# Fused Flamingo layer pair on one core: weight loads of the context stage issued by GpSimd, ternary halves laid out as 2 KB runs in DRAM

## Chip, core and metric

The kernel runs on one core of one Trainium2 chip. The metric is the device time of one execution in microseconds, the median of several runs; lower is better. The profile is of one execution.

## What is computed

Two gated layers over x (4 x 512 x 512) with a context of 4 x 1024 x 512:

```
x = x + tanh(g_xattn[0]) * L0_xattn(layernorm(x), ctx, mask)       # softmax readout of the context
x = x + tanh(g_ffn[0])   * L0_ffn(layernorm(x), router, wg, wu, wd)  # 8 experts, ternary weights
x = x + tanh(g_xattn[1]) * L1_xattn(layernorm(x), ctx, Wq, Wk, Wv, Wo)  # 16 heads
x = x + tanh(g_ffn[1])   * L1_ffn(layernorm(x), w1, b1, w2, b2)      # 8 experts, gelu
```

What the change touches is the preparation of the first feed-forward's weights, 3 matrices of 512 x 512 for each of 8 experts:

```
def _weight_quant(w):
    s = 1.0 / jnp.clip(jnp.mean(jnp.abs(w)), EPS, None)
    return jnp.clip(jnp.round(w * s), -1.0, 1.0) / s
xq @ wq.T
```

Each matrix is scaled by its mean magnitude, rounded to -1, 0 or 1, and needed transposed.

## The kernel before

The program is a row of phases with a barrier between them: context, readout, router, mixture, gather, query, attention, output, expert. The order within a phase is written out by hand: each engine has its own in-order list, and semaphores tie the lists together. DMAs issued by one engine go into that engine's queue.

**The context phase** (`context_phase`) is a pipeline of 64 steps s = 8q + n. Step s does one product of 12 matmuls of 128x512 on TensorE (`gemm`, L354 and L357): for n below 4 a block of K for block q of the context, else a block of V. ScalarE and VectorE (`evacuate`) take it out of PSUM as a high and a low bf16 half, and SyncE stores both (`store`, L125 keys and L128 values). Beside that, four steps of eight each split one tile of a later context block into halves (L203, L267) and transpose one (`prepare`, L342; copied out by L207 and L271). The first three blocks j = 0, 1, 2 (the weights Wk, Wv and the first context block) and j = 3 are split and transposed before the first step; `load_ctx(j, slot)` (L118) loads a block of 1 MB into one of two buffers as soon as block j-1 is split.

**The ternary weights** ride in the same steps. Matrix i (24 of them, 1 MB in float32) is loaded into slot i % 3 of `w32` (which lies in `xres`) by `load_weights(i)` on SyncE (L134). At step 2i ScalarE sums its magnitudes (`total`, L232); at step 2i+2 TensorE adds the partition sums (L365) and VectorE makes the ternary values (`ternary`, L288 to L298, the last of which increments the semaphore `cast`). After that the slot is free, and `load_weights(i+3)` waits for just this: `sp.wait_ge(cast, i - 2)`. The matrix is transposed in two halves h = 2i, 2i+1 at steps s = h+5: TensorE transposes half h (`w_transposes`, L374) into the one buffer `psW`, ScalarE copies it to buffer h % 2 of `wout` (`w_copy`, L225), and SyncE stores it to DRAM (`store_weights`, L140, 256 KB). ScalarE's `w_copy(h)` waits until the store of half h-2 has landed (semaphore `w_stored`); TensorE's transposes of half h+1 wait for `w_copy(h)`. Step s of SyncE's list is: `store(s)`, which waits for VectorE's `evacuate` of step s; `store_weights(s-5)`; then on even steps `load_weights`, which waits for `ternary`. ScalarE's step is: copy of a context transpose, `w_copy`, on even steps `total`, `evacuate`, split.

In DRAM the ternary weights lie as `wt_dram[expert, partition, matrix, k, 512]`. A half is 256 of the last 512 columns for each of the four k, so its store writes four runs of 512 B per partition. The router phase fetches an expert with 12 KB per partition (`fetch`, L768) into `wT` of the same layout, and the mixture phase multiplies with `wT[:, e, m, k, :]` as the moving operand (`weights_of`, L1134, used at L1142 and L1157).

GpSimd sets four small constants at the start of the context phase (L108 to L113) and is then idle until the next phase.

Of the kernel before, what the change touches and what calls it, by code (L numbers as in the profile page):

```python
# [5 lines left out]
F32 = mybir.dt.float32  # L6
# [5 lines left out]
P = 128  # L12
# [5 lines left out]
E = 8  # L18
# [12 lines left out]
def context_phase(nc, sem, ctx, wk, bk, wv, keys_dram, values_dram, ident, ctxN, ctxT, x, xres, moments,  # L31
# [12 lines left out]
    with ExitStack() as c:  # L44
# [60 lines left out]
        with nc.Block() as block:  # L105
            @block.gpsimd
            def _(pool):
                nc.gpsimd.memset(ident[:, :], 0.0).then_inc(ident_zero, 1)  # L108
                pool.wait_ge(ident_zero, 1)
                nc.gpsimd.affine_select(out=ident[:, :], in_=ident[:, :], compare_op=ALU.not_equal, fill=1.0,  # L110
                                        base=0, pattern=[[-1, P]], channel_multiplier=1).then_inc(ident_ready, 1)
                nc.gpsimd.memset(vst[:, :, :, 2 * HD:VW], 1.0).then_inc(ones_set, 1)
                nc.gpsimd.memset(onesf[:, :], 1.0).then_inc(onesf_set, 1)  # L113

            @block.sync
            def _(sp):
# [13 lines left out]

                def load_weights(i):
                    if i >= 3:
                        sp.wait_ge(cast, i - 2)
                    sp.dma_start(w32[:, i % 3, :, :], weights[i % 3][i // 3].rearrange("(u p) d -> p u d", p=P)  # L134
                                 ).then_inc(w_loaded[i % 3], 16)

                def store_weights(h):
                    i, r = divmod(h, 2)
                    sp.wait_ge(w_copied, h + 1)
                    sp.dma_start(wt_dram[i // 3, :, i % 3, :, r * 2 * P:(r + 1) * 2 * P],  # L140
                                 wout[:, r, :, :]).then_inc(w_stored[r], 16)
# [23 lines left out]
                load_ctx(2, 0)  # L165
                for i in range(3):
                    load_weights(i)
                load_ctx(3, 1)
                load_ctx(4, 0)
                for s in range(8 * NQ):  # L170
# [3 lines left out]
                    if (h := half_at(s)) is not None:  # L174
                        store_weights(h)
                    if (i := summed_at(s)) is not None and i + 3 < NW:
                        load_weights(i + 3)
                    for b in range(B):
# [487 lines left out]
def router_phase(nc, sem, router_w, wt_dram, means, ident, xres, moments, wT, scales, expert_of, place, dispatch_dram):  # L666
# [5 lines left out]
    with ExitStack() as c:  # L672
# [55 lines left out]
        with nc.Block() as block:  # L728
            @block.gpsimd
            def _(pool):  # L730
# [10 lines left out]
                done(nc.gpsimd.tensor_tensor(rstd[:, :], veps[:, :], half[:, :], ALU.pow))  # L741
                nc.gpsimd.memset(wT[:, E - 2:E, :, :, :], 0.0).then_inc(zero_set, 1)
                pool.wait_ge(zero_set, 1)
# [22 lines left out]
            def _(sp):  # L766
                def fetch(e):
                    sp.dma_start(wT[:, e, :, :, :].rearrange("p m k d -> p (m k d)"),  # L768
                                 wt_dram[e].rearrange("p m k d -> p (m k d)")).then_inc(w_fetched, 16)

# [3 lines left out]
                sp.dma_start(dispatch_dram.rearrange("(p n) d -> p (n d)", p=P),  # L774
                             wT[:, E - 2:E, :, :, :].rearrange("p e m k d -> p (e m k d)")[:, 0:NS * DW].bitcast(F32)).then_inc(zero_stored, 16)
                for e in range(E):
# [180 lines left out]
def mixture_phase(nc, sem, ident, wT, scales, expert_of, dispatch_dram, mixture_dram):  # L957
# [3 lines left out]
    with ExitStack() as c:  # L961
# [32 lines left out]
        with nc.Block() as block:  # L994
# [129 lines left out]
            def _(pe):  # L1124
# [7 lines left out]
                def weights_of(j):  # L1132
                    e = nc.tensor.value_load(expert_of[0:1, bass.ds(j, 1)], min_val=0, max_val=E - 1)
                    return lambda m, k: wT[:, bass.ds(e, 1), m, k, :].rearrange("p o d -> p (o d)")  # L1134

# [1095 lines left out]
def flamingo_kernel(nc, a, out):  # L2231
# [8 lines left out]
    values_dram = dram("values", (B, T, NH * VW), BF16)  # L2240
    wt_dram = dram("ternary", (E, P, 3, KC, D), BF16)
    used = []
# [5 lines left out]
    with ExitStack() as c:  # L2248
# [12 lines left out]
        with ExitStack() as moe:  # L2261
            wT = moe.enter_context(nc.sbuf_tensor("wT", [P, E, 3, KC, D], BF16))
            scales = moe.enter_context(nc.sbuf_tensor("scales", [P, 2, NT + E - 1], F32))
# [63 lines left out]
```

## Time and profile before

| | us |
|---|---|
| median of 3 runs (range) | 1882.03 (1881.41 to 1887.19) |
| profiled execution | 1875.83 |
| its span | 1874.1 |
| TensorE busy, mean granted clock | 1468.3, 0.894 |
| VectorE busy | 1261.1 |
| ScalarE busy | 955.2 |
| GpSimd busy | 387.8 |
| context phase, start to the readout's first instruction | 0 to 319.9 |

Engines: PE is TensorE's matmuls, PEld its weight loads, DVE VectorE, ACT ScalarE, POOL GpSimd, SP SyncE; "SPq" is the time that SyncE's sequencer takes for a DMA issue. A row of waits says who waited for whom. Clock and DMA share are fractions of full speed and of 16 DMA engines.

### The profile page before, as it was taken

To read this page: it belongs to the slowest core of one execution; us is meant where nothing else is said; L and a number is where in the kernel's file an instruction comes from. 1 tells how busy PE (TensorE), PEld (TensorE's weight loads), DVE (VectorE), ACT (ScalarE), POOL (GpSimd) and SP (SyncE) were. 2 spreads that over 40 slices of the span, in tenths; PEclk is the share of its full clock that TensorE was granted. 3 is DMA by queue.
4 is the path that set the end of the run, shared out by engine and by line. 5 is a ranking of instruction groups with operands and counts; after the bars stand their busy time and mean duration, and the time that the engine had idled before them with its cause. 6 is when DMAs were issued, how large, how long until landed. Compare 5 with 4: busy or idle time off the path is not lost. (4 is left out here: it accounts for less than half of the span.)

```text
span 1874.1 us, 26625 instructions
## 1 busy us (share of the span) xinstructions
PE 1468.3 (78%) x8457; PEld 806.2 (43%) x8536; DVE 1261.1 (67%) x1528; ACT 955.2 (51%) x1426; POOL 387.8 (21%) x279
## 2 busy tenths in 40 slices
PE   4777877999933574277899999999945679999996
PEld 3444443455412232142344444444412356667663
DVE  3765664655576476744999999999837867665561
ACT  4655652344324453231477676777732277666551
POOL 0000000000032002500355555555663100000000
PEclk8989889999965798577799999999977779999998
DMA  6787756000035123822042424242138277666640
GB/s 213 229 258 243 233 189 219 1 0 0 1 146 218 63 87 107 207 63 79 10 108 75 106 72 110 71 108 70 31 123 230 106 263 246 215 225 232 228 154 29
DMA packets 168979, 251.54 MB, mean 134 GB/s; under 512 B 11321, under 2 KB 86073, under 8 KB 167745
## 3 DMA queue, kind: packets, MB, share of 16 engines
q1 hardware_dynamic: 166848, 244.21, 41.4%
q0 software_dynamic: 2048, 6.33, 1.1%
q8 instruction: 41, 0.67, 0.2%
q14 instruction: 42, 0.34, 0.1%
HBM read 180.23 MB, written 70.07 MB: 134 GB/s over the span
## 5 line engine op out<-in xcount | busy, mean ns | idle before, releaser
L1607 ACT ACTIVATE t_e<-t_psE 128x512 f32<-128x512 f32 x512 | 304.4, 597 | 138.2 <-PE t_psE L1702 113.3
L1646 DVE TENSOR_REDUCE t_nmax<-t_psM 128x1 f32<-128x1024 f32 x256 | 301.4, 1212 | 19.6 <-PE t_psM L1683 19.5
L1565 POOL TENSOR_TENSOR t_low<-t_e 128x1024 bf16<-128x1024 f32 x128 | 250.0, 1955 | 201.8 <-ACT t_e L1607 188.3
L1713 PE MATMUL t_psO<-t_e,vst 128*96 128x512 bf16 x512 | 199.6, 390 | 2.5 <-POOL t_low L1565 2.5
L1702 PE MATMUL t_psE<-t_qst,kst 99*128 99x512 bf16 x512 | 195.0, 382 | 5.6 <-ACT t_e L1607 5.4
L1713 PE MATMUL t_psO<-t_low,vst 128*96 128x512 bf16 x512 | 193.1, 377 | 0.0
L1654 DVE TENSOR_TENSOR t_low<-t_e 128x1024 bf16<-128x1024 f32 x128 | 173.6, 1357 | 24.2 <-ACT t_e L1607 23.9
L1683 PE MATMUL t_psM<-kst,t_qst 96*128 96x512 bf16 x512 | 164.1, 404 | 31.7 <-DVE t_nmax L1646 22.7
L2196 PE MATMUL e_psG<-xeT,e_w1p 128*128 (+1 forms) x1536 | 172.8, 276 | 9.8 <-DVE e_hT L2140 5.2
L2211 PE MATMUL e_psO<-e_w2p,e_hT 128*128 128x512 bf16 x752 | 164.9, 379 | 0.8
L2196 PEld LDWEIGHTS e_psG<-xeT,e_w1p 128*128 128x128 bf16 x1536 | 151.7, 99 | 31.3 <-issue 6.3
L2211 PEld LDWEIGHTS e_psO<-e_w2p,e_hT 128*128 128x128 bf16 x768 | 75.2, 98 | 88.9
L354 PE MATMUL c_psG<-ctxT,c_wT 128*128 128x512 bf16 x369 | 94.6, 408 | 2.2 <-DVE c_vst L280 0.9
L357 PE MATMUL c_psG<-c_wT,ctxT 128*128 128x512 bf16 x371 | 92.7, 401 | 0.9 <-issue 0.2
L1683 PEld LDWEIGHTS t_psM<-kst,t_qst 96*128 96x128 bf16 x512 | 47.2, 99 | 106.7 <-DVE t_nmax L1646 48.3
L225 ACT COPY c_wout<-c_psW 128x1024 bf16<-128x1024 bf16 x48 | 48.7, 1015 | 83.9 <-DMA ternary<-c_wout 82.9
L1713 PEld LDWEIGHTS t_psO<-t_e,vst 128*96 128x96 bf16 x512 | 63.1, 123 | 64.8 <-POOL t_low L1565 6.3
L638 PE MATMUL a_psR<-ctxN,a_pT 128*128 (+1 forms) x375 | 85.7, 384 | 4.3 <-DVE xres L551 3.9
L2092 ACT CAST e_w2p<-xres 128x2048 bf16<-128x2048 f32 x32 | 60.7, 1897 | 53.1 <-PE e_psO L2211 36.6
L616 PE MATMUL a_psS<-ctxT,a_xT 128*128 (+1 forms) x375 | 86.5, 385 | 0.6 <-issue 0.2
L2132 DVE TENSOR_TENSOR e_w1p<-piece,e_w1p 128x2048 bf16<-128x2048 f32 x32 | 72.2, 2287 | 18.5 <-ACT e_w1p L2087 18.5
L2098 ACT ACTIVATE e_g<-e_psG,e_b1T 128x256 f32<-128x256 f32 x128 | 53.6, 470 | 60.0 <-PE e_psG L2196 39.6
(228 smaller groups left out, 2238.1 us busy)
## 6 DMA issues: line engine op xcount, KB each, us to landing
piece<-in_L_ffn_w SPq DMA_DIRECT2D x32, 1024.0 KB, 13.7
xres<-in_L_ffn_w SPq DMA_DIRECT2D x32, 1024.0 KB, 15.2
values<-c_vst SPq DMA_DIRECT2D x32, 384.0 KB, 4.8
ternary<-c_wout SPq DMA_DIRECT2D x48, 256.0 KB, 5.5
wT<-ternary SPq DMA_DIRECT2D x8, 1536.0 KB, 23.5
kst<-keys SPq DMA_DIRECT2D x96, 128.0 KB, 4.0
vst<-values SPq DMA_DIRECT2D x16, 768.0 KB, 8.3
mixed<-t_ost SPq DMA_DIRECT2D x64, 192.0 KB
```

The lines of the kernel that those rows point to most:

```text
L354: last = nc.tensor.matmul(psG[:, k, :], wT[:, 0, a, k * P:(k + 1) * P], ctxT[:, b, q * 512:(q + 1) * 512], start=(i == 0), stop=(i == 11))
L357: last = nc.tensor.matmul(psG[:, k, :], ctxT[:, a, q * 512 + k * P:q * 512 + (k + 1) * P], wT[:, 1, b, :], start=(i == 0), stop=(i == 11))
L616: last = nc.tensor.matmul(psS[:, par, h * 512:(h + 1) * 512], xT[:, par, ra * KC + k, :], ctxT[:, rb * KC + k, bass.ds(b * T + h * 512, 512)],
L1565: nc.gpsimd.tensor_tensor(low[:, slot(h, u), :, :], e32[:, slot(h, u), :, :], upper(h, u), ALU.subtract).then_inc(lo_pool, 1)
L1607: nc.scalar.activation(e32[:, slot(h, u), i, :], psE[:, i, :], ACT.Exp, scale=SC).then_inc(expd, 1)
L1646: nc.vector.tensor_reduce(nmax[:, h // G % 2, h % G, u:u + 1], banks_of(place_of_max(b, m)).rearrange("p a t -> p (a t)"), AX_X, ALU.max, ...
L1654: nc.vector.tensor_tensor(low[:, slot(h, u), :, :], e32[:, slot(h, u), :, :], upper(h, u), ALU.subtract).then_inc(lo_dve, 1)
L1683: last = nc.tensor.matmul(banks_of(place_of_max(b, m))[:, i, :], qst[0:KR, g, h % G, u * P:(u + 1) * P], kst[0:KR, g, h % G, i * 512:(i + ...
L1702: nc.tensor.matmul(psE[:, i, :], kst[:, g, h % G, k * P:(k + 1) * P], qst[:, g, h % G, :], start=True, stop=True).then_inc(scored, 1)
L1713: last = nc.tensor.matmul(psO[0:VW, h % 2, :], vst[:, g, 2 * u + i, h % G, :], part[:, i, :], start=(u == 0 and i == 0 and r == 0), stop=( ...
L2196: last = nc.tensor.matmul(psG[:, g % 4, i, :], w1p[:, ra, k, f:f + P], xeT[:, rb * KC + k, ee, :].rearrange("p o s -> p (o s)"), start=(n ...
L2211: last = nc.tensor.matmul(psO[:, m, :], hT[:, ra, k, m * P:(m + 1) * P], w2p[:, rb, k, :], start=(k == 0 and i == 0), stop=(k == FC - 1 an ...
```

## The change

The weight loads of all 24 matrices move from SyncE's list to the end of GpSimd's. GpSimd first waits until the first context block has landed (`rows_loaded[0]` at 32), issues three loads, then one for each count of `cast`, the same semaphore and count as before. SyncE's list loses them and is otherwise the same. In DRAM and in `wT` the dimension of the half stands ahead of k, so a half is 1024 values, one run of 2 KB per partition; the mixture's moving operand becomes two runs of 256 values with 1024 from one to the next.

```diff
@@ context_phase, gpsimd
+                pool.wait_ge(rows_loaded[0], 32)
+                for i in range(NW):
+                    if i >= 3:
+                        pool.wait_ge(cast, i - 2)
+                    nc.gpsimd.dma_start(w32[:, i % 3, :, :], weights[i % 3][i // 3].rearrange("(u p) d -> p u d", p=P)
+                                        ).then_inc(w_loaded[i % 3], 16)
@@ context_phase, sync
-                def load_weights(i):
-                    if i >= 3:
-                        sp.wait_ge(cast, i - 2)
-                    sp.dma_start(w32[:, i % 3, :, :], weights[i % 3][i // 3].rearrange("(u p) d -> p u d", p=P)
-                                 ).then_inc(w_loaded[i % 3], 16)
-
                 def store_weights(h):
                     i, r = divmod(h, 2)
                     sp.wait_ge(w_copied, h + 1)
-                    sp.dma_start(wt_dram[i // 3, :, i % 3, :, r * 2 * P:(r + 1) * 2 * P],
+                    sp.dma_start(wt_dram[i // 3, :, i % 3, r, :, :],
                                  wout[:, r, :, :]).then_inc(w_stored[r], 16)
...
                 load_ctx(2, 0)
-                for i in range(3):
-                    load_weights(i)
                 load_ctx(3, 1)
...
-                    if (i := summed_at(s)) is not None and i + 3 < NW:
-                        load_weights(i + 3)
@@ mixture_phase, tensor
-                    return lambda m, k: wT[:, bass.ds(e, 1), m, k, :].rearrange("p o d -> p (o d)")
+                    return lambda m, k: wT[:, bass.ds(e, 1), m, :, k, :].rearrange("p o r d -> p (o r) d")
@@ flamingo_kernel
-    wt_dram = dram("ternary", (E, P, 3, KC, D), BF16)
+    wt_dram = dram("ternary", (E, P, 3, 2, KC, D // 2), BF16)
-            wT = moe.enter_context(nc.sbuf_tensor("wT", [P, E, 3, KC, D], BF16))
+            wT = moe.enter_context(nc.sbuf_tensor("wT", [P, E, 3, 2, KC, D // 2], BF16))
```

SyncE's list from the first context load on, before (`c_rows<-in_ctx` is a context load, `xres<-in_L_ffn_w*` a weight load, `ternary<-c_wout` a half's store):

```order
L118 DMA c_rows<-in_ctx 128x4x512 [waits c_lo_done]
L134 DMA xres<-in_L_ffn_wg 128x4x512
L134 DMA xres<-in_L_ffn_wu 128x4x512
L134 DMA xres<-in_L_ffn_wd 128x4x512
L118 DMA c_rows<-in_ctx 128x4x512 [waits c_lo_done] x3
L125 DMA keys<-c_kst 128x2x512 [waits c_lo_out] x3
```

and around steps 15 to 18, before:

```order
L134 DMA xres<-in_L_ffn_wg 128x4x512 [waits c_cast]
L128 DMA values<-c_vst 128x1536 [waits c_lo_out]
L140 DMA ternary<-c_wout 128x4x256 [waits c_w_copied]
L118 DMA c_rows<-in_ctx 128x4x512 [waits c_lo_done]
L125 DMA keys<-c_kst 128x2x512 [waits c_lo_out]
L140 DMA ternary<-c_wout 128x4x256 [waits c_w_copied]
L134 DMA xres<-in_L_ffn_wu 128x4x512 [waits c_cast]
```

The same two places of SyncE's list in the changed kernel:

```order
L124 DMA c_rows<-in_ctx 128x4x512 [waits c_lo_done] x4
L131 DMA keys<-c_kst 128x2x512 [waits c_lo_out] x4
```

```order
L134 DMA values<-c_vst 128x1536 [waits c_lo_out]
L140 DMA ternary<-c_wout 128x1024 [waits c_w_copied]
L124 DMA c_rows<-in_ctx 128x4x512 [waits c_lo_done]
L131 DMA keys<-c_kst 128x2x512 [waits c_lo_out]
L140 DMA ternary<-c_wout 128x1024 [waits c_w_copied]
```

GpSimd's list in the changed kernel, from the last constant to the fifth load (the row of `c_onesf` was the last of this phase before):

```order
L113 MEMSET c_onesf 128x128
L118 DMA xres<-in_L_ffn_wg 128x4x512 [waits c_rows_loaded0]
L118 DMA xres<-in_L_ffn_wu 128x4x512
L118 DMA xres<-in_L_ffn_wd 128x4x512
L118 DMA xres<-in_L_ffn_wg 128x4x512 [waits c_cast]
L118 DMA xres<-in_L_ffn_wu 128x4x512 [waits c_cast]
```

The loads left SyncE's list, where each stood between a store and the next step's stores, and stand alone in GpSimd's. The lists of TensorE, VectorE and ScalarE hold the same instructions in the same order.

## Rows read from the trace of the kernel before

**Rows 1.** Waits, 0 to 400 us: who waited for whom, total us, times, longest
```profile
ACT c_wout L225 <- DMA ternary<-c_wout: 82.9, 30, 9.0
...
PE c_psW L374 <- ACT c_wout L225: 48.3, 16, 5.1
```
**Rows 2.** Timeline of ScalarE, evacuations of steps 8 and 40: start, us, what
```profile
74.18 0.69 ACT L214 ACTIVATE c_kst<-c_psG,c_bias 128x512 bf16<-128x512 f32 x1 [1.07 <-PE c_psG L354]
...
231.83 0.68 ACT L214 ACTIVATE c_kst<-c_psG,c_bias 128x512 bf16<-128x512 f32 x1
```
**Rows 3.** Stretches: length, busy PE, PEld, DVE, ACT, POOL, then clock, DMA share, GB/s
```profile
111.00:150.00 39.00, 30.23 (x195) 16.56 (x197) 24.96 (x34) 23.69 (x30) 0.00 (x0) 0.91 0.78 243
150.00:192.00 42.00, 30.66 (x203) 17.27 (x205) 25.06 (x34) 24.25 (x33) 0.00 (x0) 0.92 0.76 242
```
**Rows 4.** Timeline of SyncE from 148 us, steps 23 to 28
```profile
148.19 0.37 SPq L134 DMA_DIRECT2D xres<-in_L_ffn_wu  x1
148.79 0.35 SPq L128 DMA_DIRECT2D values<-c_vst  x1
149.19 0.43 SPq L140 DMA_DIRECT2D ternary<-c_wout  x1
149.66 1.35 SPq L118 DMA_DIRECT2D c_rows<-in_ctx  x1
...
159.99 0.47 SPq L140 DMA_DIRECT2D ternary<-c_wout  x1
165.84 0.47 SPq L140 DMA_DIRECT2D ternary<-c_wout  x1
...
173.40 1.40 SPq L140 DMA_DIRECT2D ternary<-c_wout  x1
```
**Rows 5.** Timeline of ScalarE, `w_copy` of steps 25 and 28; in brackets idle before
```profile
157.15 1.01 ACT L225 COPY c_wout<-c_psW 128x1024 bf16<-128x1024 bf16 x1 [6.21 <-DMA ternary<-c_wout]
...
168.86 1.01 ACT L225 COPY c_wout<-c_psW 128x1024 bf16<-128x1024 bf16 x1 [0.99 <-DMA ternary<-c_wout]
```
**Rows 6.** Timeline of TensorE from 149 us
```profile
149.71 0.61 PE L374 MATMUL c_psW<-ident,xres 128*128 128x128 bf16 x8
150.16 2.75 PE L354 MATMUL c_psG<-ctxT,c_wT 128*128 128x512 bf16 x12
...
153.19 0.33 PE L365 MATMUL c_psA<-c_absum,c_onesf 128*128 128x1 f32 x2
158.31 1.01 PE L374 MATMUL c_psW<-ident,xres 128*128 128x128 bf16 x8 [4.78 <-ACT c_wout L225]
159.54 3.61 PE L354 MATMUL c_psG<-ctxT,c_wT 128*128 128x512 bf16 x11 [0.22 <-DVE c_kst L277]
```
**Rows 7.** DMA to landing, line 140 (ternary halves, 256 KB, runs of 512 B)
```profile
DMA to landing us min/median/max: 2.6/5.5/10.3
```
**Rows 8.** DMA to landing, tile c_kst (keys, 256 KB, runs of 1 KB)
```profile
DMA to landing us min/median/max: 2.1/4.2/10.4
```
**Rows 9.** DMA to landing, line 134 (weight loads, 1 MB)
```profile
DMA to landing us min/median/max: 5.5/6.2/12.0
```
**Rows 10.** Timeline of the start, SyncE and ScalarE
```profile
12.98 0.38 SPq L118 DMA_DIRECT2D c_rows<-in_ctx  x1
...
18.43 2.18 ACT L203 CAST ctxN<-c_rows 128x512 bf16<-128x512 f32 x4 [1.33 <-DMA c_rows<-in_ctx]
...
29.28 2.18 ACT L203 CAST ctxN<-c_rows 128x512 bf16<-128x512 f32 x4 [5.61 <-DMA c_rows<-in_ctx]
...
36.67 1.91 ACT L232 ACTIVATE ctxT<-xres 128x2048 bf16<-128x2048 f32 x1
```
**Rows 11.** GpSimd issues a DMA of 128 rows, timeline at 596 us
```profile
596.29 0.97 POOL L759 DMA_INDIRECT dispatch<-r_disp,place  x1 [0.30 <-issue]
```
**Rows 12.** Tile g_rows: GpSimd's DMA issues, VectorE's work beside them, ns min/median/max
```profile
L1192 POOL DMA_INDIRECT g_rows<-mixture,place x16: 947/1104/1234, 736.8 to 757.9; - x16
L1199 DVE SCALAR_TENSOR_TENSOR xres<-g_rows,gates,xres x16: 733/750/753, 740.2 to 761.8; 128x512 f32<-128x512 f32 x16
```
**Rows 13.** Timeline: load of matrix 11, the sum that needs it, its last ternary pass
```profile
129.08 0.37 SPq L134 DMA_DIRECT2D xres<-in_L_ffn_wd  x1
...
139.87 1.91 ACT L232 ACTIVATE ctxT<-xres 128x2048 bf16<-128x2048 f32 x1
...
154.61 1.23 DVE L298 TENSOR_SCALAR xres<-xres 128x2048 bf16<-128x2048 f32 x1
```
**Rows 14.** Tiles xres and c_rows: VectorE's work on 2048 and on 512 float32, ns
```profile
L294 DVE TENSOR_SCALAR xres<-xres x24: 1226/1227/1227, 50.1 to 274.5; 128x2048 f32<-128x2048 f32 x24
...
L267 DVE TENSOR_TENSOR ctxN<-c_rows,ctxN x40: 677/681/693, 10.5 to 259.9; 128x512 bf16<-128x512 f32 x40
```
**Rows 15.** Groups of the mixture, 620 to 736 us: busy, mean ns, idle before
```profile
L1142 PE MATMUL m_psG<-wT,m_xT 128*128 x178 | 45.2, 395 | 16.8 <-ACT m_xT L1026 14.9 <-DVE m_prod L1084 1.0 <-issue 0.7
```

More of the change, by code:

```diff
@@ L741, in _ @@
                 done(nc.gpsimd.tensor_tensor(rstd[:, :], veps[:, :], half[:, :], ALU.pow))
-                nc.gpsimd.memset(wT[:, E - 2:E, :, :, :], 0.0).then_inc(zero_set, 1)
+                nc.gpsimd.memset(wT[:, E - 2:E, :, :, :, :], 0.0).then_inc(zero_set, 1)
                 pool.wait_ge(zero_set, 1)
@@ L767, in fetch @@
                 def fetch(e):
-                    sp.dma_start(wT[:, e, :, :, :].rearrange("p m k d -> p (m k d)"),
-                                 wt_dram[e].rearrange("p m k d -> p (m k d)")).then_inc(w_fetched, 16)
+                    sp.dma_start(wT[:, e, :, :, :, :].rearrange("p m r k d -> p (m r k d)"),
+                                 wt_dram[e].rearrange("p m r k d -> p (m r k d)")).then_inc(w_fetched, 16)
                 sp.wait_ge(consts, ROWS_ZERO)
@@ L774, in _ @@
                 sp.dma_start(dispatch_dram.rearrange("(p n) d -> p (n d)", p=P),
-                             wT[:, E - 2:E, :, :, :].rearrange("p e m k d -> p (e m k d)")[:, 0:NS * DW].bitcast(F32)).then_inc(zero_stored, 16)
+                             wT[:, E - 2:E, :, :, :, :].rearrange("p e m r k d -> p (e m r k d)")[:, 0:NS * DW].bitcast(F32)).then_inc(zero_stored, 16)
                 for e in range(E):
```

## Prediction

> **What bounds the kernel now.** I read the waits first. The largest of the context stage is ScalarE's `w_copy`, which waits 82.9 us for stores of ternary halves to land; behind it TensorE waits 48.3 us, in 16 waits, for ScalarE to empty the one transpose buffer [rows 1]. The reader is to see that a DMA's landing, not its traffic, holds up the matmuls. Next the pace: steps 8 to 40 take 231.83 - 74.18 = 157.65 us, so a pair of steps (one matrix) takes 9.85 us [rows 2]. The stretches say what is not the bound: per 39 to 42 us TensorE is busy 30, VectorE 25, ScalarE 24, and the DMA engines 0.76 to 0.78 [rows 3].
>
> Then the timeline of one stall. At 148.19 SyncE issues a weight load of 1 MB, at 148.79 a store of values, at 149.19 a ternary half [rows 4]. That half lands when `w_copy` of step 25 starts, at 157.15: 7.96 us later, of which ScalarE sat idle 6.21 [rows 5]. TensorE's next transposes come at 158.31, after 4.78 us idle, and run at half rate (1.01 us where 0.61 stood before; then 3.61 us for 11 matmuls against 2.75 for 12) [rows 6]. So each long wait costs about 1.5 us more in clock.
>
> This closes into a loop per parity of step. Odd steps: from the start of `w_copy` at 157.15 to the next odd store at 159.99 go 2.84 us (copy, evacuation by ScalarE and VectorE, issue), so a pair takes at least L + 2.84, with L the time from issue to landing. By the pace, L is 9.85 - 2.84 = 7.0 on average. Even steps also hold the 1.9 us `total`: from the store of 165.84 the wait ends at 168.86 (L = 3.0), and the next even store is issued 4.54 us later, at 173.40, so L + 4.54 = 7.6 at the shortest [rows 4, 5]. TensorE's own floor per pair is 2 x 2.75 + 2 x 0.61 + 0.33 + 0.61 (one context transpose set on average) = 7.66 us [rows 6].
>
> **The change, part by part.** *The load leaves SyncE's queue.* SyncE's issues of 0.37 us are off the path: it mostly waits for VectorE. What counts is the place of the load in the queue. In the example it stood 1 us ahead of the half and held the odd half up. A load's minimum to landing is 5.5 us, a half's 2.6 and a keys store's 2.1 [rows 7 to 9]; at the start five transfers of 1 MB, issued from 12.98, are all in by 29.28, so 1 MB occupies the DMA engines for at most 16.3 / 5 = 3.3 us [rows 10]. In a queue of its own it can no longer delay the stores by that whole; it can share the engines with them. No row shows two queues at once, so I bound it. Best: no interference, odd L = 7.0 - 3.3 = 3.7. Worst: it goes first all the same, 7.0. In between, with equal turns, store and half (about 2 us of work together) take twice their time: 3.7 + 2 = 5.7.
>
> *Runs of 2 KB.* Keys with 1 KB runs land 0.5 us sooner at best than halves of the same 256 KB with 512 B runs [rows 7, 8]. I take 0.5 us off each L; bounds 0 and 1 us (what another halving of the run, twice over, would give at the same step). Odd L becomes 3.2 to 6.5, I take 5; even L, which was 3.0 when no load was in flight, becomes 2.5 to 4.5 (the load is now in flight beside it as often as before), I take 4.0. One even half in four still has a 1 MB context load close by (149.66 in [rows 4]), which stays in SyncE's queue: 0.3 us on the mean.
>
> *New pace.* Odd: 5 + 2.84 = 7.8. Even: 4.0 + 4.54 + 0.3 = 8.9. TensorE: 7.7. The even loop sets it: 8.9 against 9.85, 0.95 us less for each of 23 pairs, 22 us. The clock's recovery lies inside this, since both loops run beside TensorE. Bounds of the pair: 7.7 (50 us gained) and 9.85 (none).
>
> *The start.* ScalarE splits block 3 at 29.28 after 5.61 us of idleness, because its load stood behind three weight loads in one queue; its work before ended at 23.7 [rows 10]. Now GpSimd waits for the first context block (landed by 18.43) and only then issues its loads, so block 3, already queued, has the engines nearly alone: about 18.2 + 3.3 + 1 = 22.5. The 5.6 us go, and the first `total`, at 36.67 before, moves to 31. Matrix 0 is issued at 18.4; with 1 to 5 us of descriptor work and equal turns it is there by 18.4 + 3 + 6.6 = 28. Late next is matrix 1, needed some 8 us after. Bounds: 0 to 5.6; I take 5.6.
>
> *GpSimd's issue work.* A DMA of 128 rows takes it 0.97 us and 0.30 to the next [rows 11]. A weight matrix has 512 rows. The cost lies between 1 us (per instruction) and 4 x 1.27 = 5.1 (per row); I take 3. GpSimd is otherwise idle, so only the load's landing moves: from 6.2 [rows 9] to about 3 + 1.6 x 3.3 + 2 = 10 us. Matrix 11's load was issued at 129.08 and needed at 139.87, 10.8 us later [rows 13]; at the faster pace the margin is near 10. I count nothing, and the range has it. GpSimd's waiting load stands alone in its list: behind it are only further loads, and the phase's end.
>
> The Trainium skill, in "SBUF — State Buffer", section "Who interferes with whom", adds that a GpSimd DMA's descriptors are written through a port pair that VectorE holds for the whole of a two-port instruction. This case's rows agree that the three ternary passes are of that kind: 2048 values in 1227 ns, where 512 in a two-input pass take 681 [rows 14]. By that rule up to 3.7 us would come on a load's landing; that is taken up in the third rival.
>
> *The mixture's operand* is two runs of 256 instead of one of 512; its matmuls take 395 ns on average, mostly at half clock [rows 15]. A 512 B run is still long against an element; I count 0. If each of the 276 cost 10 ns more it were 3 us. The router's fetch of 12 KB runs is the same.
>
> Sum: 22 + 5.6 = 27.6 us off the profiled execution's 1875.83, so 1848. That one stands 6.2 us below the median of the runs shown, 1882.03, so I predict 1882 - 27.6 = 1854.4, rounded to 1855.
>
> **Rivals.** *A: the wait only changes its name.* The 16 DMA engines are the same, 0.78 busy; with the load in a second queue every store takes as long as before, even L rises to 5.3 (loop 9.85), and only the start is won: 1876. For it: even stores, fast until now because the load had drained when they came, would meet it later. Against: one L in two is measurably the load's. The Trainium skill says the same in "DMA: Bandwidth & Descriptors", "Issuing engines are not separate DMA queues": spreading DMAs over engines saves only issue time. That section's rule is about bandwidth; the stall here is one of order, and no row so far shows two queues together.
>
> *B: nothing.* The start's 5.6 us are eaten because matrix 0 or block 4 comes late by as much, and the loop stays: 1882. For it: the same 5 MB must come in before step 2 or so. Against: matrix 0's margin of 3 us above.
>
> *C: the loads come late, and it is slower.* Place: ScalarE's `total`, which stands ahead of the evacuation. Matrix i+3 is loaded when the ternary values of i are done; from its sum to its own ternary values go a pair and some 6 us (139.87 to 154.61 + 1.23 = 155.84 [rows 13]), so three pairs are at least L_w + 6 + one pair: pair >= (L_w + 6) / 2. With L_w = 6.2 this was 6.1, with 10 it is 8. If GpSimd needs 5.1 us, is held up by a full ternary block of 3.7, and the load then takes equal turns (6.6) plus 2: 17.4, pair 11.7, 1.85 x 23 = 43 us more, less the start: 1919. It decides from L_w = 13.7 on. Against: beside VectorE's two-input work GpSimd's issues grew only from 0.97 to 1.1 us, and VectorE's own 750 ns did not grow [rows 11, 12].
>
> **Chances.** Forecast 0.62 (its own range 1834 to 1868), A 0.16, B 0.08, C 0.14, most of C between 1885 and 1919. No change is what lies within 0.3% of 1882, 5.6 us, about what a measurement here can tell. Faster: 0.62 and most of A, 0.76. Same: B and the rest of A, 0.11. Slower: 0.13. The range reaches from a pair of 8.0 us to the edge of B: 1834 to 1880.
>
> **What would show it.** Right: `w_copy`'s wait for the ternary store falls from 82.9 to some 35 us, TensorE's wait behind it from 48 to under 20; steps 8 to 40 take about 142 us; block 3 is split by 24 us; halves' shortest landing is 2.1; ScalarE's `total` waits for no weight load. Wrong: that wait stays above 70 (A), `total` waits on `xres` loads for more than 15 us (C), VectorE's passes stretch or wait on GpSimd, GpSimd's issue takes above 5 us, or the readout's first instruction is not 20 us or more ahead of 319.9.

## The result and the profile after

The changed kernel takes 1888.43 us (median of 14 runs, 1883.38 to 1892.84) against 1880.38 us (14 runs, 1873.06 to 1887.19) of the kernel before on the same chip: ratio 1.0042, 95% interval [1.0028, 1.0056]. It is slower by 0.42%, where 1855 us had been forecast, and outside the range. The profiled executions have spans of 1883.2 and 1874.1 us.

The page of the changed kernel. The weight loads now form most of queue q0:

```profile
span 1883.2 us, 26703 instructions
...
DMA packets 144402, 251.54 MB, mean 134 GB/s; under 512 B 11320, under 2 KB 61496, under 8 KB 143168
## 3 DMA queue, kind: packets, MB, share of 16 engines
q1 hardware_dynamic: 135744, 219.04, 36.4%
q0 software_dynamic: 8576, 31.49, 5.8%
```

The kernel before had 86073 packets under 2 KB; now there are 61496. So both edits do what they say. Next the waits, 0 to 400 us (who waited for whom; total us, times, longest), beside [rows 1]:

```profile
POOL xres L118 <- DVE xres L294: 220.8, 21, 25.1
ACT c_wout L221 <- DMA ternary<-c_wout: 89.7, 28, 9.0
...
PE c_psW L370 <- ACT c_wout L221: 56.1, 18, 6.4
PEld c_psW L370 <- issue: 51.2, 16, 6.5
...
POOL xres L118 <- DMA c_rows<-in_ctx: 16.0, 1, 16.0
```

Both waits that were to shrink grew: 82.9 to 89.7 us and 48.3 to 56.1 us. GpSimd's 220.8 us is idleness of an engine with nothing else to do. Now ScalarE's timeline (start, length, instruction, in brackets the idle time before it): the first evacuation, those of steps 8, 24, 40 and 48, and the end of the phase, beside [rows 2]:

```profile
30.49 1.91 ACT L228 ACTIVATE ctxT<-xres 128x2048 bf16<-128x2048 f32 x1
...
33.31 0.69 ACT L210 ACTIVATE c_kst<-c_psG,c_bias 128x512 bf16<-128x512 f32 x1 [0.82 <-PE c_psG L350]
...
70.04 0.69 ACT L210 ACTIVATE c_kst<-c_psG,c_bias 128x512 bf16<-128x512 f32 x1 [1.50 <-PE c_psG L350]
...
152.91 0.69 ACT L210 ACTIVATE c_kst<-c_psG,c_bias 128x512 bf16<-128x512 f32 x1 [0.57 <-PE c_psG L350]
...
235.22 0.69 ACT L210 ACTIVATE c_kst<-c_psG,c_bias 128x512 bf16<-128x512 f32 x1
...
278.52 0.69 ACT L210 ACTIVATE c_kst<-c_psG,c_bias 128x512 bf16<-128x512 f32 x1 [1.25 <-PE c_psG L350]
```

The phase starts 6.64 us earlier (first evacuation at 33.31, 39.95 before) and its first `total` comes at 30.49 instead of 36.67. Then it gives that back and more: a pair of steps takes (235.22 - 70.04) / 16 = 10.32 us where it took 9.85. Over steps 8 to 48 it is 10.42 against 9.86. The readout's first instruction comes at 327.47 instead of 319.86, 7.6 us late; after it the two executions differ by 1.5 us. The stretches (columns as in [rows 3]):

```profile
111.00:150.00 39.00, 30.24 (x195) 16.67 (x194) 24.97 (x34) 21.82 (x30) 2.99 (x4) 0.88 0.69 216
150.00:192.00 42.00, 34.04 (x210) 17.99 (x209) 24.96 (x34) 24.88 (x32) 2.62 (x4) 0.86 0.72 236
```

The DMA engines are less busy than before (0.69 and 0.72, where they had 0.78 and 0.76), and the phase is slower, so their busy share is not what limits it. The granted clock fell from 0.91 and 0.92 to 0.88 and 0.86. That does not tell of the loss: layout_only, an experiment below that takes the same time as the kernel before, had 0.89 and 0.83 in these stretches.

**One load and the stores behind it.** GpSimd, then SyncE, then ScalarE of the changed kernel, 147 to 157 us, the same place as [rows 4, 5]:

```profile
147.89 0.75 POOL L118 DMA_DIRECT2D xres<-in_L_ffn_wu  x1 [9.01 <-DVE xres L294]
```
```profile
149.37 0.34 SPq L134 DMA_DIRECT2D values<-c_vst  x1
149.75 0.43 SPq L140 DMA_DIRECT2D ternary<-c_wout  x1
150.22 0.77 SPq L124 DMA_DIRECT2D c_rows<-in_ctx  x1
```
```profile
156.38 1.01 ACT L221 COPY c_wout<-c_psW 128x1024 bf16<-128x1024 bf16 x1 [2.78 <-DMA ternary<-c_wout]
```

What each queue moved then, counted from the trace's DMA records (packets that started in each 0.5 us; a load of 1 MB is 256 packets of 4 KB, a values store 128 of 3 KB, a half 128 of 2 KB):

```
from us   load (q0, 4 KB)   values (q1, 3 KB)   2 KB (q1)
149.0            4                 0                0
149.5           17                 0                0
150.0           21                 0                0
150.5            6                 0                0
151.0           41                 0                0
151.5           46                 0                0
152.0           29                 0                0
152.5           37                 0                0
153.0           40                 1                0
153.5           15                44                0
154.0            0                64                5
154.5            0                19               69
```

The reader is to see the column of the values store. It was issued at 149.37 to an empty queue and moved nothing until 153.46, when 94% of the load's packets had started. The two queues don't take turns here; the later one waits for nearly the whole earlier transfer. A longer stall begins with the load of 96.88; the half of 97.59 stands behind it (GpSimd, SyncE, ScalarE, TensorE):

```profile
96.88 0.75 POOL L118 DMA_DIRECT2D xres<-in_L_ffn_wd  x1 [11.12 <-DVE xres L294]
```
```profile
97.21 0.34 SPq L134 DMA_DIRECT2D values<-c_vst  x1
97.59 0.43 SPq L140 DMA_DIRECT2D ternary<-c_wout  x1
```
```profile
105.91 1.01 ACT L221 COPY c_wout<-c_psW 128x1024 bf16<-128x1024 bf16 x1 [7.52 <-DMA ternary<-c_wout]
```
```profile
107.06 1.01 PE L370 MATMUL c_psW<-ident,xres 128*128 128x128 bf16 x8 [6.26 <-ACT c_wout L221]
```

Between 100.0 and 101.5 us not one data packet of SyncE's queue moved, with that half waiting in it; from its issue to the copy that needed it went 8.3 us. This place shows the other order too. The values store of 97.21 was issued 0.33 us behind the load, yet its packets went first: they began at 98.05, 0.84 us after issue, and the load's only at 99.36. So the issue that comes first need not win. It looks as if what counts is whose packets are ready first, and GpSimd's take longer to be ready. In the changed kernel four stores issued 0.33 us behind a load, to an empty queue, overtook it like this (first packet after 0.83 to 0.84 us); the ten issued 0.99 to 2.19 us behind one did not, and waited 2.7 to 4.8 us.

**The same for all halves.** From each half's issue to the `w_copy` that reuses its buffer (halves 2 to 43), sorted by whether a weight load was issued within 3 us ahead of it; worked out from the timelines of each trace (the experiments named here follow below):

```
                     behind a load     other halves    w_copy to issue,   issue to w_copy,
                      us      n         us      n      halves even/odd    halves even/odd
before               6.19    17        4.69    25        4.12 / 5.01        5.73 / 4.86
layout_only          6.74    17        4.20    25        4.18 / 5.28        5.78 / 4.68
changed kernel       7.23    17        4.61    25        4.10 / 5.34        6.27 / 5.06
act_loads            6.50    19        4.91    23        3.69 / 4.80        6.18 / 5.08
load_late_sync       7.49     8        4.10    34        5.67 / 4.58        4.32 / 5.18
load_late_pool       7.81     5        4.35    37        5.63 / 4.59        4.24 / 5.29
small_loads          3.36    21        3.61    21        5.06 / 4.71        3.31 / 3.66
small_loads_pool     3.33    23        3.45    19        5.01 / 4.82        3.28 / 3.48
half_first           7.28    31        6.88    11        2.68 / 2.09        6.85 / 7.50
half_first_all       7.18    30        6.54    12        2.78 / 2.13        6.63 / 7.36
half_first_late      7.87    25        7.50    17        1.21 / 1.97        8.15 / 7.29
after_half_first     8.15    19        7.58    23        1.21 / 1.64        8.11 / 7.56
```

Against the kernel before, the halves that are not behind a load are as fast (4.61 and 4.69), and the 17 behind one take 1.04 us more. Against layout_only, which differs by the move and the start's order alone, both groups are slower, by 0.49 and 0.41 us. Even halves go out at odd steps. For each parity the last two columns add up to a pair of steps by their definition, since they measure from one `w_copy` to the one two halves later.

### The profile page after: what moved, and what is told of

It reads as the page before. It is cut to its first block and busy times, and to the rows that moved or that the text cites. A ratio compares the mean times of both kernels' runs of the same rounds, so it can differ in the third digit from the quotient of the medians.

```text
span 1883.2 us, 26703 instructions
## 1 busy us (share of the span) xinstructions
PE 1480.3 (79%) x8535; PEld 808.0 (43%) x8536; DVE 1260.6 (67%) x1528; ACT 954.5 (51%) x1426; POOL 405.3 (22%) x303
## 5 line engine op out<-in xcount | busy, mean ns | idle before, releaser
L353 PE MATMUL c_psG<-c_wT,ctxT 128*128 128x512 bf16 x384 | 98.7, 415 | 0.0
L221 ACT COPY c_wout<-c_psW 128x1024 bf16<-128x1024 bf16 x48 | 48.7, 1016 | 90.8 <-DMA ternary<-c_wout 89.7
L1679 PEld LDWEIGHTS t_psM<-kst,t_qst 96*128 96x128 bf16 x512 | 47.2, 99 | 106.5 <-DVE t_nmax L1642 48.3
L2128 DVE TENSOR_TENSOR e_w1p<-piece,e_w1p 128x2048 bf16<-128x2048 f32 x32 | 72.2, 2287 | 18.4 <-ACT e_w1p L2083 18.4
```

Of the source, the lines that this page charges most:

```text
L353: last = nc.tensor.matmul(psG[:, k, :], ctxT[:, a, q * 512 + k * P:q * 512 + (k + 1) * P], wT[:, 1, b, :], start=(i == 0), stop=(i == 11))
L1679: last = nc.tensor.matmul(banks_of(place_of_max(b, m))[:, i, :], qst[0:KR, g, h % G, u * P:(u + 1) * P], kst[0:KR, g, h % G, i * 512:(i + ...
L2128: nc.vector.tensor_tensor(half1(1, p), raw1(p), half1(0, p), ALU.subtract).then_inc(w1_lo, 1)
```

## The experiments

All ratios are to the kernel before on the same chip, with 95% intervals.

**The three parts of the change, one at a time.** layout_only is the kernel before with the 2 KB runs and nothing else:

```diff
-                    sp.dma_start(wt_dram[i // 3, :, i % 3, :, r * 2 * P:(r + 1) * 2 * P],
+                    sp.dma_start(wt_dram[i // 3, :, i % 3, r, :, :],
```

> The kernel before with only the 2 KB runs in DRAM; SyncE issues the weight loads as before. Theory Q (the second queue costs the time: once GpSimd's load runs, a half issued by SyncE waits for it and then shares the engines with it): the layout is harmless or helps, shortest landing of a half 2.1 instead of 2.6 us, 0 to 8 us faster than before. Rival R (the layout costs: the two-run operand in the mixture, or the stores in DRAM): this one alone is 4 to 10 us slower, with the mixture longer or w_copy's wait longer.

Measured: 1880.27 us, 1.0005 [0.9993, 1.0016], with a shortest landing of 2.4 us. The layout is worth nothing in time. Its saving on the DMA engines is real but small: a 512 B packet takes 27 ns and a 2 KB packet 84 ns, so the 512 packets of a half took 13.8 us of engine time and its 128 packets take 10.8, spread over 16 engines.

ctx3_first is the kernel before with the fourth block's load ahead of the three weight loads, the start's order alone:

```diff
                 load_ctx(2, 0)
+                load_ctx(3, 1)
                 for i in range(3):
                     load_weights(i)
-                load_ctx(3, 1)
```

> The kernel before with one line moved: context block 3 is loaded ahead of the first three weight matrices, all by SyncE. Theory Q: the start's gain needs no second queue; ScalarE splits block 3 near 24 us instead of 29.28 and the whole is 4 to 7 us faster than before, pairs at 9.85. Rival (the start's gain is eaten by the steps behind it, as the changed kernel's steps 0 to 8 suggest, which took 2.5 us longer): within 2 us of before.

Measured: 1873.34 us, 0.9975 [0.9962, 0.9988], first evacuation at 33.2 us (33.3 in the changed kernel). All of the start's gain comes from this order; it needs no second queue.

pool_only is the changed kernel with the old layout (runs of 512 B):

```diff
-                    sp.dma_start(wt_dram[i // 3, :, i % 3, r, :, :],
+                    sp.dma_start(wt_dram[i // 3, :, i % 3, :, r * 2 * P:(r + 1) * 2 * P],
```

> The changed kernel with the old layout (runs of 512 B); GpSimd issues the loads. Theory Q: the start is won (6.6 us, first evacuation near 33.3 us), the pairs of steps are longer than before (over 10.3 us against 9.85), and since 512 B packets take turns with packets of 4 KB it is slower than the changed kernel, 8 to 20 us above before. Rival R: without the layout it is faster than before by the start's 6 us.

Measured: 1887.23 us, 1.0045 [1.0027, 1.0063]. So the slowdown is there without the layout, though this kernel has the start's new order too. Theory Q expected it to be slower than the changed kernel as well; it isn't, so 512 B packets beside the load's 4 KB ones cost no more here than 2 KB packets. Without the move the parts give 1.0005 x 0.9975 = 0.9980; with it 1.0042; the move costs 0.62%, some 12 us (products of ratios from different chips).

**Is it GpSimd's work, or the load's traffic?** In small_loads (on the kernel before) and small_loads_pool (the same edit on the changed kernel) matrices 3 and up load only 32 B per partition; the weights' values are then wrong, and the lists of instructions the same:

```diff
+                        nc.gpsimd.dma_start(w32[:, i % 3, 0, 0:8], weights[i % 3][i // 3][0:P, 0:8]).then_inc(w_loaded[i % 3], 16)
+                        continue
```

> The kernel before, but from the fourth weight matrix on only 32 B per partition are loaded, of the first 128 rows (the ternary values of those 21 matrices are then not the reference's; nothing else is left out). It takes the 1 MB loads away and leaves every wait. Theory Q/L (a half's landing sets the pace and the load ahead of it in the queue is what makes it late): a half lands in about 3.5 us, w_copy's wait for it under 25 us in all, pair of steps 7.7 to 8.3 us, 30 to 50 us faster. Rival D (the pace comes from the engines' own order, and the landing is only the name of the wait): pair stays above 9.3 us, less than 12 us faster.

> The changed kernel with the same small loads issued by GpSimd (the ternary values of 21 matrices are not the reference's). Theory Q (what costs in the changed kernel is the traffic of GpSimd's queue beside the stores): with no traffic it is as fast as the same edit on the kernel before, or a few us faster through the start and the layout, 0.970 to 0.982 of before. Rival G (GpSimd's issue work or its hold on VectorE costs): it stays 8 us or more behind the other small-loads kernel.

Measured: 1840.06 us, 0.98 [0.9777, 0.9822], and 1833.99 us, 0.9748 [0.9731, 0.9766]. With next to nothing to move, GpSimd's loads cost nothing: the second is faster, by about the start's gain. So GpSimd's waits and the place of its list are not the cause; what costs comes with the large transfer. The edit takes away more than bytes: a load is 16 packets instead of 256, and its issue takes 0.54 us instead of 0.75. Whether this work costs something by itself is answered by load_late_pool below, which keeps all of it and is as fast as its counterpart on SyncE. The load's traffic is worth 38 us in all. The waits of small_loads, against [rows 1]:

```profile
ACT c_wout L227 <- DMA ternary<-c_wout: 61.0, 34, 9.0
...
PE c_psW L376 <- ACT c_wout L227: 20.7, 16, 2.1
```

Even with the traffic gone TensorE's wait isn't below the 20 us that the forecast named, and `w_copy`'s is far above the 25 of this expectation. The landing of a half holds `w_copy` up with no load in its way, too; of its 82.9 us the loads account for 22.

**Another second queue.** act_loads issues the loads from ScalarE, after its evacuation of the step, with start and layout of the change:

```diff
+                def load_weights(i):
+                    if i >= 3:
+                        act.wait_ge(cast, i - 2)
+                    act.dma_start(w32[:, i % 3, :, :], weights[i % 3][i // 3].rearrange("(u p) d -> p u d", p=P)
+                                  ).then_inc(w_loaded[i % 3], 16)
...
+                        if s % 2 == 1 and (i := summed_at(s - 1)) is not None and i + 3 < NW:
+                            load_weights(i + 3)
```

> The loads in ScalarE's own queue: as in the changed kernel they leave SyncE's queue, but the descriptors are made as SyncE's are and the packets are 2 KB like the half's; issued behind the evacuation of step 2i+3, first three at the same place as block 4. Layout and start as in the changed kernel. Theory Q1 (the loss comes from GpSimd's queue alone: 4 KB packets, two thirds of the engines, and stores that start 4 us late): a half no longer stands behind the load, pair under 9.4 us, 8 to 20 us faster than before. Theory Q2 (any second queue costs, since the load then meets both stores): pair 9.9 to 10.4, within 5 us of before. ScalarE's issues add 24 x 0.4 us beside waits.

Measured: 1876.48 us, 0.9978 [0.9964, 0.9992]: what the start and the layout give with all loads in SyncE's queue (0.9980). A second queue as such is neither gain nor loss. Here too SyncE's next store, issued 0.6 to 1.3 us behind a load while its queue was idle, waited 3.4 to 4.9 us for its first packet, with 82% to 94% of the load's packets gone (18 loads). Theory Q2's time is what came. ScalarE paid 21.2 us of waits for VectorE's cast, and the time is the same even so.

What is left between 0.9978 and 1.0042 no run isolates. One difference is when the load's packets begin. GpSimd issues the load 0.30 us after VectorE's cast has ended, SyncE and ScalarE 0.03 us after it. From issue to the first packet, on idle engines, SyncE's loads take 1.04 to 1.06 us (9 in the kernel before) and ScalarE's 1.04 to 1.06 (13). GpSimd's take 1.45 to 1.64 (6 in the changed kernel); four more take 2.47 to 2.61, each behind 118 to 121 packets of the values store that overtook it. The loads' landing in the changed kernel (against [rows 9]: 5.5/6.2/12.0) has a median 0.8 us later:

```profile
DMA to landing us min/median/max: 5.6/7.0/12.1
```

The second difference is the packets: 4 KB from GpSimd, 2 KB from ScalarE. The third is ScalarE's own order, with its waits for the cast. The later start is therefore not shown to be the cause, and the table speaks against its being all of it: from issue to `w_copy` the halves of act_loads take as long as the changed kernel's (6.18 and 5.08 against 6.27 and 5.06). What is shorter is the way from `w_copy` to the issue, 3.69 and 4.80 us against 4.10 and 5.34.

**Put the load behind the half.** If the load's place is the cause, issuing it later should help in either queue. load_late_sync has every DMA in SyncE's queue, with start and layout of the change:

```diff
                     store(s)
                     if (h := half_at(s)) is not None:
                         store_weights(h)
-                    if (i := summed_at(s)) is not None and i + 3 < NW:
+                    if s and (i := summed_at(s - 1)) is not None and i + 3 < NW:
                         load_weights(i + 3)
```

> The kernel before with the layout and the start of the change, all issues by SyncE, and each weight load one place later in SyncE's list: behind the next step's keys or values store and ternary half, instead of ahead of them. Theory 1 (order within a queue: a transfer of 1 MB ahead of a half holds it up by its own 3 us): the half's mean from issue to the w_copy that waits for it falls from 5.73 us in the even halves to below 4.5, and the time comes to some 1860. Theory 2 (the load's traffic is paid wherever it stands; the next even store, 3 us later, now has it ahead): the other parity's mean rises by what the first falls, and the time stays near ctx3_first's, 1873.

load_late_pool is the changed kernel with the same order:

```diff
                         pool.wait_ge(cast, i - 2)
+                    if i >= 4:
+                        pool.wait_ge(w_copied, 2 * i - 7)
+                        pool.wait_ge(lo_out, 2 * i + 2)
```

> The changed kernel, with GpSimd's waits made later: from the fifth matrix on its load waits also for the copy into wout and the evacuation of the next step, so it is issued at the same moment as that step's stores instead of 1 to 2 us ahead. Theory 1 (SyncE's DMA that is issued just behind a GpSimd load starts its packets 3.2 us after issue instead of 1.05, and this is what made the change slower): with the load issued beside or behind, the half's first packets follow 1.1 us after issue, the mean from issue to the next w_copy of the even halves falls from 6.27 us to below 5.3, and the time comes to 1870 or less. Theory 2 (equal turns by packet between a queue of 4 KB packets and one of 2 KB packets, wherever the load stands): the wait moves to the other parity and the time stays at 1884 to 1890. Against load_late_sync, which has the same order in one queue, the difference is the queue's own.

Measured: 1869.4 us, 0.9954 [0.9936, 0.9972], and 1867.43 us, 0.9949 [0.993, 0.9967]. Two added waits make the changed kernel 0.9% faster (0.9949 / 1.0042 = 0.9907), some 17 us. The halves that stand behind a load fell from 17 to 5, and the even halves' mean from issue to `w_copy` from 6.27 to 4.24 us. With the same order the two queues give the same time: their intervals nearly coincide. So in this order neither GpSimd's queue nor its 4 KB packets cost anything. For load_late_sync, Theory 1's 4.5 us came (4.32) but not its 1860: against ctx3_first and the layout (0.9980) the later load is worth 0.26%, and the two intervals overlap. For load_late_pool, Theory 1 holds in its outcome, but its words were too narrow: the late start isn't special to GpSimd's queue (act_loads has it), and the 4 stores that still found a load 1.0 to 4.0 us ahead of them and their own queue empty waited 1.6 to 4.5 us, with 80% to 97% of its packets gone. Theory 2 had a part that is right: the other parity's mean rose, from 5.06 to 5.29, less than the first fell. From `w_copy` to issue it went the other way, 5.63 us where it was 4.10 for the even halves. The landing of halves and of keys in load_late_pool:

```profile
DMA to landing us min/median/max: 2.4/4.0/10.3
```
```profile
DMA to landing us min/median/max: 2.1/2.7/10.7
```

In the changed kernel these medians were 6.0 and 4.7. Yet `w_copy`'s wait stays at 88.9 us in all; TensorE's behind it fell:

```profile
ACT c_wout L224 <- DMA ternary<-c_wout: 88.9, 29, 8.7
...
PE c_psW L373 <- ACT c_wout L224: 44.3, 20, 5.9
```

**Put the half ahead of its step's store.** half_first is the kernel before with two lines swapped. A half is ready when `w_copy` ends, and SyncE's list held it behind the step's keys or values, so that 3 to 4 us went by:

```diff
-                    store(s)
                     if (h := half_at(s)) is not None:
                         store_weights(h)
+                    store(s)
```

> The kernel before with SyncE's two stores of a step swapped: the ternary half is issued before the keys or values, so it no longer waits for VectorE's evacuation of that step. Theory L (the loop over a half's landing sets the pace, so what counts is how early the half is issued): from the start of w_copy to the issue 1.4 us instead of 2.84 (odd) and 4.54 (even) and up to 4 us less behind the ternary passes; pair 7.7 to 8.8 instead of 9.85, TensorE's wait behind w_copy falls from 48 us to under 20, 20 to 45 us faster. Rival D (the DMA engines' total work sets the pace): w_copy's wait moves to another line and the time stays within 5 us.

Measured: 1868.83 us, 0.9943 [0.9927, 0.9958]. From `w_copy` to issue go 2.68 and 2.09 us instead of 4.12 and 5.01, and `w_copy`'s wait falls to 72.2 us. The 10 us gained are half of the least that Theory L forecast, and TensorE's wait behind `w_copy` is 38.5 us, not under 20. Of 2.2 us by which the halves go out earlier, 1.9 come back as a longer way to the next `w_copy` (7.18 us where it was 5.29), and the pair of steps falls by 0.28. Between 60 and 260 us SyncE still waits 70.4 us for VectorE's cast (for a load) ahead of halves that could go.

after_half_first is the same swap in the changed kernel.

> The changed kernel with SyncE's two stores swapped, the half ahead of the keys or values. With no weight load in SyncE's list it can then issue the half as soon as w_copy is done, 3 to 5 us ahead of the load that cast lets go. Theory L (how early the half is issued against the load counts): the half is through before the load's packets start, w_copy's wait falls under 45 us, pair 8.6 to 9.3, 15 to 30 us faster than before. Rival (GpSimd's load holds the stores back whatever their order): 0 to 5 us faster than the changed kernel, still slower than before.

Measured: 1852.38 us, 0.9861 [0.9846, 0.9877], as Theory L forecast, though `w_copy`'s wait isn't under its 45 us. Its waits:

```profile
ACT c_wout L221 <- DMA ternary<-c_wout: 60.2, 15, 8.5
...
PE c_psW L370 <- ACT c_wout L221: 33.3, 13, 4.2
```

Here the change is worth something: more than layout, start and swap add up to (1.0005 x 0.9975 x 0.9943 = 0.9923). half_first_all and half_first_late ask why. Both have layout, start and swap with every DMA in SyncE's queue; the second also has the later load of load_late_sync.

```diff
                     if (h := half_at(s)) is not None:
                         store_weights(h)
                     store(s)
-                    if (i := summed_at(s)) is not None and i + 3 < NW:
+                    if s and (i := summed_at(s - 1)) is not None and i + 3 < NW:
                         load_weights(i + 3)
```

> The kernel before with the layout, the third context load ahead of the weight loads, and the ternary half issued ahead of the keys or values store of its step: what after_half_first does, but with every DMA in SyncE's queue. If GpSimd's queue only costs (theory 1), this is at least as fast as after_half_first, 1852 or less. If the parts add up (layout 0, start -0.25%, half first -0.57%), 1864, and then GpSimd's queue, harmful by itself, is worth 0.6% once the half no longer waits behind the store: by taking the wait for cast out of SyncE's list, where 70.4 us of it stood ahead of the halves.

> half_first_all with each weight load one place later in SyncE's list, so that the wait for cast no longer stands ahead of a half. If that wait is what kept half_first_all from the time of after_half_first, this reaches 1852 without GpSimd's queue. If the load's traffic ahead of the next half costs as much as the wait did, it stays within 0.3% of half_first_all.

Measured: 1863.47 us, 0.9916 [0.9899, 0.9934], the sum of its parts; and 1852.77 us, 0.9858 [0.9838, 0.9879], the same as after_half_first. SyncE's waits in half_first_all, 0 to 330 us:

```profile
SPq L134 <- DVE xres L298: 81.1, 21, 4.3
SPq L125 <- DVE c_kst L277: 48.5, 27, 7.3
```

Its first row, the load's wait for the cast, stands ahead of the next half in the list. In half_first_late and after_half_first that row is gone, in the one by an order, in the other by GpSimd's list, and from `w_copy` to issue the even halves take 1.21 us in both, where they took 2.78. So what a second issuing engine buys is that SyncE doesn't stand at the load's wait; in the change as made that was of little use, because the half was held by the keys or values store in front of it. In both kernels fewer halves also stand behind a load (25 and 19, where half_first_all has 30), and no run separates this from the wait. These two are the fastest kernels of the study that load all weights, 1.4% below the kernel before, and aren't told apart.

Not tried: a third or fourth buffer for the halves, by which `w_copy` would wait for an older store.

## Why the prediction was wrong

- *The start*: right. 5.6 us were forecast, 6.6 came; ScalarE split block 3 at 23.49. The cause is the order alone (ctx3_first).
- *Layout 0.5 us per L*: wrong, nothing. The minimum of a half's landing went from 2.6 to 2.4, not to 2.1, and the time did not move.
- *GpSimd's issue 3 us*: 0.75 us measured (748 to 997 ns), below the lower bound of 1. Its first packet comes 0.4 us later than SyncE's, or some 1.5 where a store overtakes it, and the load lands at 7.0 at the median, not at 10. The Trainium skill's rule on the shared port pair ("SBUF — State Buffer", "Who interferes with whom") had been priced at up to 3.7 us. GpSimd's rows show no such stretch, but they hardly test it: each load is issued 0.30 us after the last of VectorE's three ternary passes has ended.
- *The load leaves SyncE's queue*: this is the step that failed. "In a queue of its own it can no longer delay the stores by that whole; it can share the engines with them." It delayed them by that whole: a store issued 1 to 2.2 us behind a load found 80% to 97% of the load's packets gone before its own first (10 of 21 loads, 2.7 to 4.8 us). Of the three cases named there, 3.7, 5.7 and 7.0 us, the worst, "it goes first all the same", is what happened. The forecast took 5; the measured mean went from 5.73 to 6.27. That worst case leaves the start's gain alone, and act_loads has just this time. Why the move to GpSimd costs another 0.62% stays open. It hangs on the moment of issue, since the same loads in the same queue cost nothing once two waits make them later.
- *The loop's terms*: both read from one instance. Odd L was taken as 9.85 - 2.84 = 7.0 us; the mean distance from copy to issue is 4.12, and the mean L 5.73. Even L was taken as 3.0; the mean is 4.86. So the prize was smaller than it looked. The even steps, which set the forecast's pace, had no prize at all: the forecast added 4.0 + 4.54 + 0.3 = 8.9 us, where the means before are 4.86 + 5.01 = 9.87 and after 5.06 + 5.34 = 10.40. The forecast also held the distance fixed. The runs show that the two terms lean on each other: load_late_pool's even halves have L 2.03 us shorter than the changed kernel's and the distance 1.53 longer, half_first has the distance 2.2 shorter and L 1.9 longer. A gain in one is no gain of the pair.
- *Mixture's operand 0*: right. Its matmuls, 627 to 746 us, against [rows 15]:

```profile
L1138 PE MATMUL m_psG<-wT,m_xT 128*128 x184 | 45.3, 391 | 16.7 <-ACT m_xT L1022 14.5 <-issue 1.2 <-DVE m_prod L1080 1.0
```

- *Rivals*. A (the wait only changes its name) had the mechanism and missed the 0.62% of the move: 1876 forecast, which is what act_loads gives. Its sign, a wait of `w_copy` above 70 us, came too (89.7). C had the sign and not the cause: `total` waited 1.9 us for a load, VectorE's passes did not stretch. The Trainium skill says in "DMA: Bandwidth & Descriptors", "Issuing engines are not separate DMA queues", that such a move saves only issue time; I set it aside as a rule on bandwidth while the stall was one of order. The runs agree with it: the loads in ScalarE's queue give 0.9978, in SyncE's 0.9980. They show besides that a transfer whose packets have begun mostly keeps its lead across the queues.

The sum, as it came: start -6.6, from the first evacuation to the readout +14.3 (279.9 to 294.2 us), the rest +1.5; together +9.1 in the spans. The pair grew by 0.52 us (mean L 5.29 to 5.67, mean distance 4.57 to 4.72), 12 us over 23 pairs. Why q1's packets wait for q0's is not settled: an engine that takes transfers in the order in which they become ready would do it, and so would descriptors already handed down. No run here separates these.

## What to carry to other kernels

Another issuing engine gives a transfer another place in a list of waits, not another place in line at the DMA engines: a small urgent store issued 1 us behind a 1 MB load waits for nearly all of it, in whichever queue. Only a store issued 0.33 us behind GpSimd's load still overtook it. So look first at the moment of issue, put what somebody waits for ahead of what nobody needs soon, and keep waits for late semaphores out of the list that issues it. And take the terms of a loop from the mean over all its turns, ask of each whether it stays when another shrinks, and don't read them from the longest stall.

## What the runs showed of the hardware

- Two queues at once are not always served by equal turns: with a 1 MB load under way, the first packet of another queue's store, issued 1 to 2.2 us (GpSimd's loads) or 0.6 to 1.3 us (ScalarE's) behind it, came when 80% to 97% or 82% to 94% of it had started. With 32 B per partition in place of the load it came 0.87 to 1.17 us after issue (18 stores of small_loads_pool).
- The lead doesn't always go to the transfer that was issued first: four values stores issued 0.33 us behind a GpSimd load in the changed kernel moved their first packet after 0.83 to 0.84 us, and the load's first came only at 2.47 to 2.61 us.
- Once both run, packets can alternate: from 29 to 31 us in the changed kernel each 0.5 us holds 30 to 32 packets of 4 KB from one and 31 to 33 of 2 KB from the other, so the queue with the larger packets gets two thirds.
- The same 1 MB load moves as 4 KB packets (159 ns) from GpSimd and as 2 KB packets (84 ns) from SyncE or ScalarE. Its issue takes 0.75 us against 0.37, and with nothing ahead of it its first packet comes at 1.45 to 1.64 us against 1.04 to 1.06.
- Fewer, larger packets lowered the engines' busy share from 0.78 to 0.70 (layout_only, 111 to 150 us) and changed no time.
